# A GpSimd program in a new order, maxima between score pairs, and a weight quantization spread over more steps, in a cross-attention and FFN kernel

## What is computed

```python
B, S, E, T, H, D, I = 8, 512, 256, 1601, 16, 16, 704
x = x + attention(layernorm(x), ctx, ctx)       # 16 heads of 16, softmax over T keys, biases on q, k, v, o
def fp4(x):                                     # along the last dim, blocks of 16
    scale = max(max(abs(block)) / 6, 1e-12)
    return nearest of {0, .5, 1, 1.5, 2, 3, 4, 6} to abs(block / scale), with its sign, * scale
def lin(x, w): return fp4(x) @ fp4(w).T
n = layernorm(x)
x = x + lin(silu(lin(n, w_gate)) * lin(n, w_up), w_down)
```

## Time and profile before

| | before |
|---|---|
| median of 3 runs | 1806.91 us (1804.79 to 1809.01) |
| profiled execution | 1806.17 us |
| its span in the trace | 1804.4 us |
| mean granted TensorE clock | 0.97 of full speed |
| TensorE (PE) busy | 1666.5 us, 92% |
| VectorE (DVE) busy | 1422.4 us, 79% |
| ScalarE (ACT) busy | 1131.0 us, 63% |
| GpSimd (POOL) busy | 562.2 us, 31% |

### The profile page before, as it was taken

One profiled execution on the slowest core, in us unless ns is written; L12 is line 12 of the kernel. 1 busy time (PEld: TensorE's weight loads), 2 busy tenths in 40 slices (PEclk: granted clock), 3 DMA queues, 4 the chain that ended last, 5 costly groups with the idle time before them and its releaser, 6 DMA issues.

```text
span 1804.4 us, 26956 instructions
## 1 busy us (share of the span) xinstructions
PE 1666.5 (92%) x9408; PEld 660.9 (37%) x9408; DVE 1422.4 (79%) x2077; ACT 1131.0 (63%) x2293; POOL 562.2 (31%) x673
## 2 busy tenths in 40 slices
PE   5798889999998999989999999989999899989958
PEld 2332234334432344333443334423343334323325
DVE  5778888878786887969788788878879697798447
ACT  2366667666676667666676666766677666666731
POOL 4327530532126220343205421162202532012204
PEclk8899999999998999999999999999999999999979
DMA  6644332232324313252331423243132422300000
GB/s 157 145 77 124 71 74 43 67 95 51 61 43 115 79 39 59 48 123 52 63 55 50 106 57 61 43 106 81 38 57 57 93 46 49 57 7 10 13 21 12
DMA packets 106482, 117.51 MB, mean 65 GB/s; under 512 B 23140, under 2 KB 87660, under 8 KB 106348
## 3 DMA queue, kind: packets, MB, share of 16 engines
q1 hardware_dynamic: 101808, 111.93, 29.3%
q10 hardware_dynamic: 4540, 3.87, 0.9%
HBM read 76.78 MB, written 30.16 MB: 59 GB/s over the span
## 4 chain that ended last, share of the span: by engine, by line
PE 77%; DVE 10%; ACT 5%; issue 4%; POOL 1%; DMA 0%; SPq 0%; ACTq 0%; POOLq 0%; DVEq 0%
PE pvb L824 20%; PE st L795 19%; PE mx L809 10%; PE misc L725 7%; PE misc L697 5%; DVE cmx L1051 4%; PE misc L690 4%; ACT prob L976 3%; PE misc L745 3%; PE misc L737 2%; PE misc L676 2%; PE misc L711 1%; PE misc L733 1%; PE misc L766 1%; DVE ht L1080 1%
## 5 line engine op out<-in xcount | busy, mean ns | idle before, releaser
L976 ACT ACTIVATE prob<-st 128x512 f32<-128x512 f32 (+1 forms) x1584 | 863.7, 599 | 385.3 <-PE st L795 382.8
L1051 DVE TENSOR_REDUCE cmx<-mx 128x2 f32<-128x1024 f32 x768 | 905.7, 1219 | 216.1 <-PE mx L809 212.8
L795 PE MATMUL st<-qstack,kstack 112*128 112x512 bf16 (+1 forms) x1584 | 500.0, 389 | 53.8 <-ACT prob L976 44.0
L824 PE MATMUL pvb<-prob,vv 128*32 128x512 f32 (+1 forms) x3328 | 446.9, 609 | 0.6 <-ACT prob L976 0.6
L795 PEld LDWEIGHTS st<-qstack,kstack 112*128 112x128 bf16 (+1 forms) x1584 | 128.6, 99 | 516.3 <-issue 247.0
L809 PE MATMUL mx<-kstack,qstack 48*128 48x512 bf16 (+1 forms) x2048 | 255.6, 339 | 29.5 <-DVE cmx L1051 16.4
L1306 POOL TENSOR_TENSOR ht<-ht,rh 128x352 f32<-128x352 f32 (+1 forms) x78 | 57.3, 759 | 462.2 <-DVE rh L1027 462.2
L725 PE MATMUL misc<-wguT,rowsT 128*128 128x352 f32 x456 | 154.3, 460 | 0.0
L1298 POOL TENSOR_TENSOR ht<-ht,mt 128x352 f32<-128x352 f32 (+1 forms) x140 | 124.6, 913 | 74.1 <-DVE mt L1208 60.7
L809 PEld LDWEIGHTS mx<-kstack,qstack 48*128 48x128 bf16 x2048 | 58.2, 94 | 203.4 <-issue 134.3
L1312 POOL TENSOR_TENSOR cin<-cin 128x400 f32<-128x400 f32 (+1 forms) x60 | 58.3, 972 | 233.2 <-ACT cin L916 233.2
(11 more groups left out here) (182 smaller groups left out, 1556.7 us busy)
## 6 DMA issues: line engine op xcount, KB each, us to landing
kstack<-scr_k SPq DMA_DIRECT2D x384, 100.1 KB, 4.3
scr_k<-cin SPq DMA_DIRECT2D x48, 300.0 KB, 3.9
qstack<-scr_q SPq DMA_DIRECT2D x372, 32.0 KB, 1.8
cin<-ctx_in SPq DMA_DIRECT2D x16, 512.0 KB, 5.3
scr_q<-qp SPq DMA_DIRECT2D x16, 384.0 KB, 4.5
scr_k<-cin SPq DMA_DIRECT2D x16, 300.8 KB, 4.9
xn<-x SPq DMA_DIRECT2D x8, 512.0 KB, 4.0
cin<-ctx_in SPq DMA_DIRECT2D x16, 256.0 KB, 5.5
```

The source lines that it names most:

```text
L795: mm(score_bank(it, n, h)[0:KROWS[kt], :], kstack[:, hd, KOFF[kt]:KOFF[kt] + KROWS[kt]], qstack[:, hd, :], start=True, stop=True).then_inc ...
L824: last = mm(pvb[2 * D * h:2 * D * (h + 1), :], vv[0:w, kt, (HG * g + h) // 2, D * (h % 2):D * (h % 2 + 2)], prob[0:w, n % 2, h, :], start= ...
L976: activate(prob[0:KROWS[kt], n % 2, 2 * pair + h, :], score_bank(it, n, 2 * pair + h)[0:KROWS[kt], :], ACT.Exp, scale=SCALE).then_inc(exp_ ...
L1051: v.tensor_reduce(cmx[:, g % 2, h0:h0 + 2, at:at + 1], products, op=ALU.max, axis=AX.X).then_inc(max_free, 1)
```

## The change

Three things change.

1. **`POOL_WORK`.** Key piece 2's split moves from behind `xround` 0 to behind q0, piece 3's too: the order is k0, k1, q0, k2, k3, `xround` 0, k4, q1, `xround` 1, k5, k6, k7, where it was k0, k1, q0, `xround` 0, k2, k3, k4, `xround` 1, q1, k5, k6, k7.
2. **TensorE's step.** In a step with no job on its first side, the first maxima product is issued between the two score pairs.
3. **Weight quantization.** `weight_scales` is cut in two: `weight_maxima` (the block maxima, with the waits) and `weight_scales` (the rest), each with its own table of steps; GpSimd gets tables of its own. Pieces 0 and 1 get maxima and scales in steps 12 to 15, GpSimd scales them in 14 and 16 and rounds them in 18 and 20. Transposes "wT" all stand on the first side, in the pairs of steps 21 and 22, 24 and 25, 30 and 31, 35 and 36, 40 and 41, 45 and 46.

```diff
-    24: ([("gate", 2, "late"), ("wT", 0, "once")], []),
-    25: ([("gate", 3, "late"), ("wT", 1, "once")], []),
+    21: ([("gate", 1, "late"), ("wT", 0, "once")], [("nm", 2, "att")]),
+    22: ([("up", 0, "late"), ("wT", 1, "once")], []),
+    24: ([("gate", 2, "late"), ("wT", 2, "once")], []),
+    25: ([("gate", 3, "late"), ("wT", 3, "once")], []),
...
-W_SCALE_AT = {17: 0, 19: 1, 28: 2, 31: 3, 38: 4, 41: 5}
-W_POWER_AT = {20: 0, 22: 1, 30: 2, 33: 3, 40: 4, 43: 5}
+W_AMAX_AT = {12: 0, 14: 1, 24: 2, 27: 3, 33: 4, 39: 5}
+W_SCALE_AT = {13: 0, 15: 1, 25: 2, 28: 3, 34: 4, 40: 5}
+W_POWER_AT = {17: 0, 20: 1, 26: 2, 31: 3, 37: 4, 42: 5}
+W_SCALED_AT = {14: 0, 16: 1, 25: 2, 28: 3, 34: 4, 40: 5}
+W_ROUND_AT = {18: 0, 20: 1, 26: 2, 31: 3, 37: 4, 42: 5}
 POOL_WORK = {
-    0: [("late", "bias", 0)], 10: [("early", "k", 0)], 11: [("early", "k", 1)], 12: [("early", "q", 0)], 13: [("late", "xround", 0), ("early", "k", 2)],
-    14: [("early", "k", 3)], 15: [("early", "k", 4)], 16: [("late", "xround", 1), ("early", "q", 1)], 17: [("early", "k", 5)], 18: [("early", "k", 6)], 19: [("early", "k", 7)],
+    0: [("late", "bias", 0)], 10: [("early", "k", 0)], 11: [("early", "k", 1)], 12: [("early", "q", 0), ("early", "k", 2)], 13: [("early", "k", 3)],
+    14: [("late", "xround", 0), ("early", "k", 4)], 16: [("early", "q", 1), ("late", "xround", 1)], 17: [("early", "k", 5)], 18: [("early", "k", 6)], 19: [("early", "k", 7)],
...
                     for job in jobs(it, n, 0):
                         shared(job)
+                    products = maxima(it, n)
+
+                    between = 1 if has_att and not jobs(it, n, 0) else 0
+                    for job in products[:between]:
+                        pair_products(job)
                     if has_att:
                         scores(n, 1)
-                    products = maxima(it, n)
-                    for job in products[:2]:
+                    for job in products[between:2]:
                         pair_products(job)
...
-                def weight_scales(p):
-                    w = raw_piece(p)[0]
-                    aw, sw, rw = piece_scales(p)
+                def weight_maxima(p):
+                    w, aw = raw_piece(p)[0], piece_scales(p)[0]
                     dve.wait_ge(s_wraw[p % 2], 16 * (p // 2 + 1))
                     if p >= 2:
                         dve.wait_ge(wq_done, p - 1)
                     w_linked(v.tensor_reduce(aw, blocks(w), op=ALU.max, axis=AX.X, apply_absolute_value=True))
+
+                def weight_scales(p):
+                    aw, sw, rw = piece_scales(p)
                     w_linked(scaled(sw, aw))
```

More of the change, by code:

```diff
@@ L98 @@
     26: ([("up", 2, "late")], []),
-    27: ([("up", 3, "late"), ("wT", 2, "once")], [("hqT", 0, "late")]),
-    28: ([("gate", 4, "late"), ("wT", 3, "once")], [("hqT", 1, "late")]),
+    27: ([("up", 3, "late")], [("hqT", 0, "late")]),
+    28: ([("gate", 4, "late")], [("hqT", 1, "late")]),
     29: ([("down0", 0, "late")], []),
-    30: ([("down", 0, "late")], []),
-    31: ([("gate", 5, "late")], []),
+    30: ([("down", 0, "late"), ("wT", 4, "once")], []),
+    31: ([("gate", 5, "late"), ("wT", 5, "once")], []),
@@ L104 @@
     32: ([("up", 4, "late")], [("hqT", 2, "late")]),
     33: ([("up", 5, "late")], [("hqT", 3, "late")]),
-    34: ([("gate", 6, "late"), ("wT", 4, "once")], [("nm", 3, "att")]),
-    35: ([("down0", 1, "late"), ("wT", 5, "once")], []),
-    36: ([("down", 1, "late")], []),
-    37: ([("gate", 7, "late"), ("wT", 6, "once")], [("hqT", 4, "late")]),
-    38: ([("up", 6, "late"), ("wT", 7, "once")], [("hqT", 5, "late")]),
+    34: ([("gate", 6, "late")], [("nm", 3, "att")]),
+    35: ([("down0", 1, "late"), ("wT", 6, "once")], []),
@@ L111 @@
+    36: ([("down", 1, "late"), ("wT", 7, "once")], []),
+    37: ([("gate", 7, "late")], [("hqT", 4, "late")]),
+    38: ([("up", 6, "late")], [("hqT", 5, "late")]),
     39: ([("up", 7, "late")], []),
-    40: ([("down0", 2, "late")], []),
-    41: ([("down", 2, "late")], []),
+    40: ([("down0", 2, "late"), ("wT", 8, "once")], []),
+    41: ([("down", 2, "late"), ("wT", 9, "once")], []),
     42: ([("v", 0, "early")], []),
-    43: ([("v", 1, "early")], [("hqT", 6, "late"), ("wT", 8, "once")]),
@@ L116 @@
-    44: ([("v", 2, "early")], [("hqT", 7, "late"), ("wT", 9, "once")]),
-    45: ([("down0", 3, "late")], []),
-    46: ([("down", 3, "late")], []),
+    43: ([("v", 1, "early")], [("hqT", 6, "late")]),
+    44: ([("v", 2, "early")], [("hqT", 7, "late")]),
+    45: ([("down0", 3, "late"), ("wT", 10, "once")], []),
+    46: ([("down", 3, "late"), ("wT", 11, "once")], []),
     47: ([("v", 3, "early")], [("nm", 0, "early")]),
-    48: ([("v", 4, "early")], [("wT", 10, "once")]),
-    49: ([("v", 5, "early")], [("wT", 11, "once")]),
+    48: ([("v", 4, "early")], []),
@@ L122 @@
+    49: ([("v", 5, "early")], []),
     50: ([("v", 6, "early")], []),
@@ L1252, in body @@
                     if it.kind == "first":
+                        if n in W_AMAX_AT:
+                            weight_maxima(W_AMAX_AT[n])
                         if n in W_SCALE_AT:
```

10 lines of the change are left out of this document (4 added, 6 removed).

## The result

| | before | after |
|---|---|---|
| median | 1807.05 us (1804.79 to 1809.01, 4 runs) | 1748.55 us (1746.5 to 1751.41, 4 runs) |
| profiled execution, its span | 1806.17, 1804.4 us | 1747.7, 1745.9 us |
| mean granted TensorE clock | 0.97 | 0.987 |
| a loop batch (six) | 212.6, 213.2, 211.0, 211.4, 211.5, 210.6 | 203.9, 204.0, 203.9, 203.9, 203.9, 203.0 |

The account below looks back on a forecast made before the run. TensorE, busy 92% of the span, was taken as the bound, with stalls and slow clock in the loops. Loops 51.4 + first batch 7 = 58.4 us off 1806.2 gives 1747.8, stated as 1747; range 1734 to 1769, chance 0.70.

Parts of the forecast that it names:

- Two stalls: Loop steps 15 and 19, where ScalarE waits for late key splits: 32.0 + 26.0 = 58.0 us over six batches.
- The ring is closed: Loops: GpSimd's second stand waits for VectorE, TensorE's maxima, ScalarE, and so for the first late piece; no size of its own.
- the second stall: Loop step 19: ScalarE stands 3.78 us before the copy of key piece 7, waiting for piece 5's split; 26.0 us over six.
- first stall: Loop step 15: ScalarE stands 4.10 us before the copy of key piece 4, waiting for piece 2's split; 32.0 us over six.
- rival 1: Loops: piece 5 stays late because `xround` 1 still precedes it; only step 15's gain and 5 come: 1769 us, chance 0.14.
- The second stall closes: Loop step 18: piece 5's split ends at 353.2 to 353.7, its copy wanted at 353.5, so within 0.3 us.
- Given back by contention: Loop steps 9 to 18: VectorE 92% busy and stretched beside GpSimd loses 1.1 us a batch (bounds 0 and 3), 6.6 for six.
- First batch +7: Steps 19 to 41 of the first batch: weight work moved earlier relieves VectorE, gaining 7 us, bounds -2 and +12.
- Between score pairs: First and last batch steps without a first-side job: earlier maxima products wait for VectorE all the same, gain 0.
- rival 2: Loop steps 11 to 18: VectorE becomes the bound, contention costs 3 to 6 us a batch: 1765 to 1780 us, chance 0.08.
- rival 4: Loop steps 11 to 18: VectorE's short instructions each wait a whole GpSimd instruction, making it slower: 1816 us, chance 0.02.
- best end of 72: Whole kernel: the forecast's best end, 58 + 12 + 2 = 72 us less, 1734 us.

Follow-up runs that it names:

- run 4: Kernel before, GpSimd's old order kept, with a third buffer kx so ScalarE waits for the split of piece j - 3: 1746.68 us in one run.
- run 8: Changed kernel with a third buffer kx and GpSimd's old order: 1738.72 us, ratio 0.962.
- run 2: Kernel before with only `xround` 0 moved, behind pieces 2 and 3; `xround` 1 still in front of q1: 1788.58 us in one run.
- run 3: Kernel before with only `xround` 1 moved, behind q1; `xround` 0 still in front of piece 2: 1786.82 us in one run.
- run 1: Kernel before with GpSimd's new order alone, nothing else of the change: 1761.95 us, ratio 0.9751.
- run 9: Changed kernel with `xround` 0 between key pieces 2 and 3 on GpSimd, two key buffers: 1752.54 us, ratio 0.9699.
- run 5: Changed kernel without a maxima product between the score pairs, the rest kept: 1751.63 us, ratio 0.9691.

## Why the prediction was right, and where it was not

- **Two stalls, 58.0 us, of which 18 slow clock.** Right. Steps 15 and 19 fell from 108.5 to 52.9 us, and runs 4 and 8 show the full 58 with the very step lengths, 4.35 and 4.07, that the prediction borrowed from batches without a stall. The shares were a little off, because the prediction took six times the waits of the first loop batch: over the six batches, from before to run 4, the time without TensorE work in these steps fell by 37.5 us (38.5 to 1.0) and TensorE's busy time, with the same instructions, by 20.6 (70.1 to 49.5). The first is the standing (forecast 39.7), the second the slow clock (forecast as the rest of 58.0, 18.3). The slow clock is only 1% of the span but a third of the gain.
- **"The ring is closed": the second stall waits on the first.** Wrong, though it moved no number. Run 2 has no first stall and an undiminished second, with GpSimd standing 4.65 us in front of `xround` 1. Of GpSimd's 6.29 us before, the first stall can account only for the difference. The same sentence was the "against" of rival 1. What spoke against that rival was only that q1 had moved in front of `xround` 1, since GpSimd now spends that wait on q1's split; run 3 shows this by itself, with step 19 at 4.50. Having called the second stall a consequence of the first, I could as well have left `xround` 1 where it was, for 27 us lost (1788.6 in run 2 against 1762.0 in run 1).
- **The second stall closes, piece 5 within 0.3 us of its time.** It closes, but piece 5 is some 0.75 late. The step that failed is "VectorE's part is ready 2.85 us after the end of step 15". It was ready at 339.88, 4.0 after that end (335.88), and GpSimd stood 0.82 us for it. Of the 1.15 us more, 0.83 is L1173, which took 1.26 us (0.43 without a split beside it), as in step 14, this time beside q1's split; the rest is that VectorE came to this step later than it did behind the stall. Then the last operation of piece 5's split took 1.22 where 0.94 is usual. Cost: 0.52 a batch, 3.1 in all.
- **Given back by contention: 1.1 us a batch.** This term was mis-sized, though inside its bounds of 0 to 3. Against the loops of run 4, which have no stall, it was 1.23 in step 14, 0.52 in step 19 and 0.13 in step 13, less 0.13 that step 15 gained: 1.7 a batch, 10.2 for six instead of 6.6, so the loops gave 47.8, not 51.4. I had spread it as "late by tenths"; most of it came at one place, where the exponent step meets the split of piece 3 (runs 4, 9). Both ends of the meeting could be read beforehand: the times of piece 3's split in the new order and of the exponent step. The Trainium skill ("GPSIMD Engine Reference", 1. Specifications) says that GpSimd shares its SBUF interfaces with VectorE and that they contend with VectorE instructions in a 2-port mode or with two SBUF inputs. The rows agree for an instruction with two inputs (L1102, 0.28 to 0.86 us). L1173, with one input, went from 0.43 to 1.13; no row shows whether it runs in such a mode. The maxima from PSUM stayed at 2.34 to 2.36.
- **First batch +7.** It gave 9.1, of it 7.9 in steps 19 to 41 (89.3 to 81.45). VectorE's busy time there was forecast at "some 74" and is 74.35; TensorE's own work at "about 69", and is 68.8. The waits of step 21 (forecast 2, found 1.79) and of step 24 (1, found 1.03) are there. Too much was set aside for the slow clock behind them: it did not come in this trace. In that of runs 8 and 9, with the same weight schedule, it came, and their first batches are 195.6, 6.6 shorter than before. So part of the 9.1 is luck too.
- **Between score pairs: 0.** Right: 0.1 in the first batch (run 5), and in the last batch what steps 6, 8 and 11 gain is nearly all taken back in steps 9 and 12, as argued: products that come earlier wait for VectorE all the same. The last batch and tail together gave 1.2, but 0.9 of it in the tail, which the change does not touch.
- The two misses, 3.6 us too much for the loops and 3.7 too little for the rest (2.1, 1.2 and 0.4), cancel. That the number came within 2 us is thus partly luck. The chance of rival 2 (3 to 6 us a batch) was fair: over half of its lower end came true. Two small slips moved nothing: by its own terms rival 4 comes to 1818, not 1816, and the 2 us in the best end of 72 have no row behind them.

## What to carry to other kernels

When a copy waits for a free buffer, look at what the engine that frees it has in its program in front of that work; a step that waits for a third engine doesn't belong there. Putting independent work first removes the stall, and a further buffer removes it too without moving anything (here 1.8 us a batch better, since the moved work met VectorE's row work). Before moving work on GpSimd, lay its new times beside VectorE's instructions that read and write SBUF, and price the ones that coincide where another engine waits for what comes behind them: the same kind of meeting cost 1.2 us in step 14 of the changed kernel and nothing in step 16 of run 4.
